# A selective-scan layer with a coupled feed-forward: gathers through DRAM, seven work slots, one gate per two phases, the norm's negated mean on ScalarE

## The chip, the cores and the metric

The kernel runs on one core of a Trainium2 chip. The metric is the device time of one execution in microseconds (us). Everything is float32. The engines are TensorE (PE), VectorE (DVE), ScalarE (ACT) and GpSimd (POOL); SyncE (SP) issues every DMA, in its own program order.

## The reference, cut to what matters

For each of 16 batch elements with 1024 time steps and 256 features: an input projection to 512 + 512 channels, a causal convolution of four taps, a selective scan with 16 states per channel, an output projection, a layer norm, three cycles of a small coupled network, and a second layer norm.

```
xi, res = split(x @ W_in.T + b_in);  xi = silu(conv4(xi) + b_conv)
proj  = xi @ W_x.T + b_x
delta = softplus(proj[:512]);  B, C = proj[512:528], proj[528:544]
h_t   = exp(-exp(A_log) * delta_t) * h_(t-1) + delta_t * B_t * xi_t     # 512 x 16 states, 1024 steps
y     = (sum_n h * C + xi * D) * silu(res)
x     = layernorm(x + y @ W_out.T + b_out)
out   = x;  3 times: out = out + coupling(out) * twist(out)
x     = layernorm(x + out)
```

## The kernel before, in words

**Tiling.** Channels lie on partitions. The 512 channels are DC = 4 blocks of 128, a block is QUAD = 4 groups of 32 channels. One *unit* handles 32 channels times 4 states, on 128 partitions (partition 32 n + i is state n of channel i), over all 1024 steps. Four units (j = 0 to 3, so 16 states) make a *phase*, four phases a block, and four blocks a *period* of 64 units, which is one batch element. There are 1024 units.

**A unit** runs through four engines. POOL makes `u_q * b_quad` into a slot of `work` (L944), ACT makes `da = exp(neg_a * delta_q)` (L721) into one of two PSUM buffers, DVE scans (L870), DVE or, for 24 units of a period, POOL two steps later multiplies by `c_quad` (L878, L951), and PE sums over the four states with the `fold` matrices into `y_sum` (L635). `work` has WORK = 5 slots, so POOL's unit t waits until PE has reduced unit t - 5. At the end of a phase DVE multiplies `y_sum` by silu(res) in `s_quad` (gate, L860); PE starts the next phase's sums (L626) only after that.

**Gathering.** The scan wants 32 channels repeated four times over the partitions. So for each phase SP copies 32 rows of `delta` and of `u = delta * xi` four times each, SBUF to SBUF (`copy_quads`, L338 and L344); three slots (COPIES) hold them. B and C go to DRAM once per period and are broadcast from there to b_quad and c_quad, 16 transfers each (L371), right at the change of period, into the buffers that the last phase still used. silu(res) comes from DRAM in four transfers per phase (L354), and the gated y goes in four transfers per phase to `yg` (L365), from where the output matmuls read.

**Around the units** run side tasks, at positions within the period written in tables: for the next batch element the projections x, r (L504, L519), the convolution v (L513), delta's projection d (L526), B and C (c); for the previous one the output matmuls o, transposes t, the network f and g, and the residual sum e. They share three PSUM banks, which a program assigns ahead (`assign_banks`); a task waits for the bank's former user. Every engine walks the same list t = FIRST ... END and does at each t its unit work and then its side tasks, strictly in order. ACT takes a task's result some positions later (X_TAKE, GELU1_AT and so on), and loads an activation table whenever the function changes (L657). `u` is made by POOL at DELTA_AT + U_LAG (L970). A norm is: DVE's bn_stats, bn_aggr and the negated mean (L846, L850, L853), then on ACT log, exp, shift and two applications (`normalise`, L665 to L676).

**SP** walks the list as well. At each t it may store y, load s_quad, copy the quads, store x1 (L420, at positions 9 and 12), reload x1 (L425), write out (L430), load x_res (L437), store res (L444), load x_feat, and the B and C loads. It waits for each one's data before it issues it, and nothing overtakes.

Of the kernel before, what the change touches and what calls it, by code (L numbers as in the profile page):

```python
# [30 lines left out]
WORK = 5  # L31
# [3 lines left out]
REDUCE_LAG = 1  # L35
# [32 lines left out]
F_AT = (0, 1, 1, 2, 3, 3, 5, 6, 7)  # L68
G_AT = (17, 19, 21)
E_AT = (59, 60, 61, 61)  # L70
# [60 lines left out]
def yg_position(g):  # L131

    return max(PHASE * (g + 1) + 1, PERIOD * (g // 16) + YG_AT)


def s_quad_position(g):

    return max(PHASE * (g - 2) + 1, yg_position(g - QUAD) if g >= QUAD else FIRST)
# [51 lines left out]
def build(nc, x, xT, weights, vectors, out):  # L190
    x1_dram = nc.dram_tensor("x1_scratch", [BATCH, SEQ, DM], F32, kind="Internal").ap()
    bc_dram = nc.dram_tensor("bc_scratch", [2 * NS, SEQ], F32, kind="Internal").ap()
    res_dram = nc.dram_tensor("res_scratch", [2, DC, P, SEQ], F32, kind="Internal").ap()

    with ExitStack() as ctx:
# [24 lines left out]
        yg = sb("yg", [P, DC, SEQ])  # L220
# [4 lines left out]
        neg_mean = sb("neg_mean", [P, 8, 2])  # L225
        log_var = sb("log_var", [P, 8, 2])
        r_std = sb("r_std", [P, 8, 2])
        shift = sb("shift", [P, 8, 2])
# [20 lines left out]
        def vs(name):  # L249
# [11 lines left out]
        bc_rows = soft[:, 0:QT]  # L261
# [18 lines left out]
        sq_in = [sem(f"s_quad_loaded{i}") for i in range(QUAD)]  # L280
        yg_in = [sem(f"yg_stored{i}") for i in range(QUAD)]
# [13 lines left out]
        o_ready, o_stat, o_mv, o_neg, o_log, o_rstd, o_shift, o_norm = (  # L295
            sem("o_" + n) for n in ("ready", "stat", "mv", "neg", "log", "rstd", "shift", "norm"))
        e_ready, e_stat, e_mv, e_neg, e_log, e_rstd, e_shift, e_norm = (
            sem("e_" + n) for n in ("ready", "stat", "mv", "neg", "log", "rstd", "shift", "norm"))
# [28 lines left out]
        def _(sp):  # L327
# [3 lines left out]
            def copy_quads(g):  # L331

                c, slot, m = g % QUAD, g % COPIES, g // QUAD
                sp.wait_ge(delta_ready, 2 * m + 2)
                if (before := g - COPIES) >= 0:
                    sp.wait_ge(da_ready, PHASE * before + PHASE)
                for n in range(QUAD):
                    sp.dma_start(delta_q[GROUP * n:GROUP * n + GROUP, slot, :],  # L338
                                 delta[GROUP * c:GROUP * c + GROUP, :]).then_inc(dq_in[slot], 16)
                sp.wait_ge(u_ready, m + 1)  # L340
                if before >= 0:
                    sp.wait_ge(dbx_ready, PHASE * before + PHASE)
                for n in range(QUAD):
                    sp.dma_start(u_q[GROUP * n:GROUP * n + GROUP, slot, :],  # L344
                                 u[GROUP * c:GROUP * c + GROUP, :]).then_inc(uq_in[slot], 16)

            def load_s_quad(g):

                b, m, c = g // 16, (g // QUAD) % DC, g % QUAD
                if g >= QUAD:  # L350
                    sp.wait_ge(yg_in[c], 64 * (g // QUAD))
                sp.wait_ge(res_stored, 16 * (DC * b + m + 1))
                for k in range(QUAD):
                    sp.dma_start(s_quad[GROUP * k:GROUP * k + GROUP, c, :],  # L354
                                 res_dram[b % 2, m, GROUP * c:GROUP * c + GROUP, QT * k:QT * k + QT]) \
                      .then_inc(sq_in[c], 16)

            def store_yg(g):

                b, m, c = g // 16, (g // QUAD) % DC, g % QUAD  # L360
                if m == 0 and c == 0 and b > 0:
                    sp.wait_ge(o_ready, 4 * b)
                sp.wait_ge(gated, g + 1)
                for k in range(QUAD):
                    sp.dma_start(yg[GROUP * c:GROUP * c + GROUP, m, QT * k:QT * k + QT],  # L365
                                 s_quad[GROUP * k:GROUP * k + GROUP, c, :]).then_inc(yg_in[c], 16)

            def load_rows(nb, j, tile, first, signal):

                for n in range(QUAD):  # L370
                    sp.dma_start(tile[GROUP * n:GROUP * n + GROUP, j, :],  # L371
                                 bc_dram[first + QUAD * j + n:first + QUAD * j + n + 1, :].partition_broadcast(GROUP)) \
                      .then_inc(signal[j], 16)

            def load_b(nb, j):
                sp.wait_ge(bc_stored, 64 * (nb + 1))
                if nb:
                    sp.wait_ge(dbx_ready, PERIOD * nb - PHASE + j + 1)
                load_rows(nb, j, b_quad, 0, b_in_)
# [17 lines left out]
            for t in range(FIRST, END):  # L397
                g, r, m = t // PHASE, t % PHASE, t // (4 * PHASE)
                if t % PERIOD == 0 and 0 <= t < UNITS:
                    load_c(t // PERIOD, 3)  # L400
# [623 lines left out]
```

## Time and profile before

| | us |
|---|---|
| median of 3 runs (4626.33 to 4634.05) | 4628.59 |
| the profiled execution | 4633.1 |
| its span, first to last instruction | 4631.3 |
| mean granted TensorE clock | 0.873 |
| busy: POOL, PE, DVE, ACT | 3648.9, 3639.7, 3565.9, 3059.8 |

The profile is of one execution. Its span is what the stages below add up to. A busy time is the time in which an engine had an instruction running. Where a row says "<-", it names what ended the idle time before the instruction.

### The profile page before, as it was taken

How to read it: one execution, taken by the hardware profiler on the slowest of the kernel's cores; microseconds unless marked ns; L12 is line 12 of the kernel's file. 1: busy time of each engine (PE TensorE's matmuls, PEld its weight loads, DVE VectorE, ACT ScalarE, POOL GpSimd, SP SyncE). 2: the span in 40 equal slices, each digit the busy share in tenths (PEclk: the TensorE clock that was granted, in tenths of full speed). 3: DMA queues.
4: the chain of work that ended last, by engine and by line, in shares of the span. 5: the costliest groups of instructions: out<-in, count | busy, mean ns of one | idle time of the engine just before them, and what ended most of it. 6: DMA issues, size and time to landing. Idle time of an engine off the chain costs nothing.

```text
span 4631.3 us, 53910 instructions
## 1 busy us (share of the span) xinstructions
PE 3639.7 (79%) x18112; PEld 1619.7 (35%) x18112; DVE 3565.9 (77%) x2784; ACT 3059.8 (66%) x3936; POOL 3648.9 (79%) x1602
## 2 busy tenths in 40 slices
PE   6668878788787877878688787887978788786765
PEld 2223343343333433343243433433333343433323
DVE  0887878888787887877788787887888788788871
ACT  2545857678585776858668485775858668585753
POOL 2987979889687887978879687887878879787871
PEclk8778988889898897988889898898988889898877
DMA  4454454634545444444634545445444634545430
GB/s 133 101 132 100 107 137 98 163 83 117 132 101 135 110 122 115 107 126 99 160 83 121 129 103 144 99 117 128 98 127 111 149 91 120 133 104 134 101 77 27
DMA packets 305603, 529.62 MB, mean 114 GB/s; under 512 B 77616, under 2 KB 210736, under 8 KB 305072
## 3 DMA queue, kind: packets, MB, share of 16 engines
q1 hardware_dynamic: 305328, 526.18, 46.4%
q8 instruction: 145, 2.38, 0.2%
q14 instruction: 130, 1.06, 0.1%
HBM read 154.67 MB, written 69.21 MB: 48 GB/s over the span
## 4 chain that ended last, share of the span: by engine, by line
ACT 26%; PE 25%; POOL 16%; SPq 11%; DVE 10%; issue 8%; DMA 3%; DVEq 0%; POOLq 0%; ACTq 0%
ACT L657 10%; POOL work L944 9%; ACT da L721 7%; PE banks L513 5%; DVE da L870 4%; POOL work L951 3%; PE banks L519 3%; SPq L371 3%; ACT big L692 3%; PE banks L504 3%; SPq L344 3%; DVE work L870 3%; SPq L338 3%; PE banks L593 3%; PE y_sum L635 3%
## 5 line engine op out<-in xcount | busy, mean ns | idle before, releaser
L944 POOL TENSOR_TENSOR work<-u_q,b_quad 128x1024 f32<-128x1024 f32 x1024 | 2394.6, 2359 | 424.6 <-DMA b_quad<-bc_scratch 194.8
L870 DVE TENSOR_TENSOR_SCAN da<-da,work 128x1024 f32<-128x1024 f32 x640 | 1465.4, 2290 | 355.8 <-ACT da L721 256.6
L721 ACT ACTIVATE da<-delta_q,neg_a 128x1024 f32<-128x1024 f32 x1024 | 1129.9, 1113 | 676.0 <-DVE work L878 572.5
L951 POOL TENSOR_TENSOR work<-work,c_quad 128x1024 f32<-128x1024 f32 x384 | 904.7, 2356 | 244.2 <-DVE work L870 242.3
L635 PE MATMUL y_sum<-work,v_all 128*32 128x256 f32 x8192 | 663.6, 430 | 417.2 <-DVE work L878 260.6
L878 DVE TENSOR_TENSOR work<-da,c_quad 128x1024 f32<-128x1024 f32 x640 | 782.4, 1223 | 211.7 <-DMA c_quad<-bc_scratch 191.0
L870 DVE TENSOR_TENSOR_SCAN work<-da,work 128x1024 f32<-128x1024 f32 x384 | 875.6, 2280 | 48.8 <-ACT da L721 48.3
L657 ACT ACT_TABLE_LOAD x575 | 737.7, 1283 | 35.9 <-DVE neg_mean L853 17.2
L635 PEld LDWEIGHTS y_sum<-work,v_all 128*32 128x32 f32 x8192 | 217.5, 116 | 894.3 <-DVE work L878 352.1
L526 PE MATMUL banks<-xi,w_all 128*128 128x512 f32 x1024 | 490.2, 629 | 15.7 <-ACT soft L816 12.7
L513 PE MATMUL banks<-xi,taps 128*128 128x512 f32 (+3 forms) x1024 | 458.1, 598 | 12.5 <-DVE big L895 11.7
L593 PE MATMUL banks<-oT,w_all 128*128 128x512 f32 x768 | 392.2, 647 | 39.0 <-ACT big L692 20.8
L504 PE MATMUL banks<-x_feat,w_all 128*128 128x512 f32 x512 | 311.0, 739 | 53.2 <-ACT xi L792 36.3
L665 ACT ACTIVATE log_var<-mean_var,eps_col 128x2 f32<-128x2 f32 x128 | 37.7, 295 | 422.7 <-DVE neg_mean L853 422.7
L526 PEld LDWEIGHTS banks<-xi,w_all 128*128 128x128 f32 x1024 | 197.0, 200 | 283.7 <-issue 254.1
L970 POOL TENSOR_TENSOR u<-delta,xi 128x1024 f32<-128x1024 f32 x64 | 151.0, 2360 | 160.8 <-DVE delta L907 160.8
L519 PE MATMUL banks<-x_feat,w_all 128*128 128x512 f32 x512 | 275.9, 672 | 1.1 <-DVE delta L907 1.1
L513 PEld LDWEIGHTS banks<-xi,taps 128*128 128x128 f32 x1024 | 189.0, 189 | 248.7 <-issue 228.7
L626 PE MATMUL y_sum<-xi,diag_d 128*32 128x256 f32 x2048 | 182.3, 431 | 116.4 <-DVE s_quad L860 116.4
L692 ACT ACTIVATE big<-banks,v_all 128x512 f32<-128x512 f32 x336 | 217.8, 684 | 58.7 <-PE banks L593 48.6
L548 PE MATMUL banks<-w_all,yg 128*128 128x256 f32 x1024 | 248.2, 386 | 5.3 <-DMA yg<-s_quad 5.3
L860 DVE TENSOR_TENSOR s_quad<-y_sum,s_quad 128x256 f32<-128x256 f32 x256 | 105.2, 411 | 161.0 <-PE y_sum L635 161.0
(71 smaller groups left out, 3542.3 us busy)
## 6 DMA issues: line engine op xcount, KB each, us to landing
delta_q<-delta SPq DMA_DIRECT2D x1024, 128.0 KB, 2.4
u_q<-u SPq DMA_DIRECT2D x1024, 128.0 KB, 2.5
res_scratch<-s_std SPq DMA_DIRECT2D x64, 512.0 KB, 3.3
s_quad<-res_scratch SPq DMA_DIRECT2D x1024, 32.0 KB, 1.9
b_quad<-bc_scratch SPq DMA_DIRECT2D x256, 128.0 KB, 3.0
c_quad<-bc_scratch SPq DMA_DIRECT2D x256, 128.0 KB, 3.9
yg<-s_quad SPq DMA_DIRECT2D x1024, 32.0 KB, 1.9
x_feat<-in_xT SPq DMA_DIRECT2D x16, 1024.0 KB, 5.5
```

The costliest lines, as they stand in the source:

```text
L504: mm = pe.matmul(banks[:, bank, :], w_in[:, k, m * P:m * P + P], x_feat[:, k, half * L:half * L + L], start=k == 0, stop=k == 1)
L513: mm = pe.matmul(banks[:, bank, to:], taps[:, m, k, :], xi[:, nb % 2, m, half * L + to - s:half * L + L - s], start=k == 3, stop=k == 0)
L519: mm = pe.matmul(banks[:, bank, :], w_in[:, k, DI + m * P:DI + m * P + P], x_feat[:, k, half * L:half * L + L], start=k == 0, stop=k == 1)
L526: mm = pe.matmul(banks[:, bank, :], w_x[:, k, m * P:m * P + P], xi[:, nb % 2, k, half * L:half * L + L], start=k == 0, stop=k == 3)
L593: mm = pe.matmul(shared, w1[:, k, m * P:m * P + P], oT[:, k, half * L:half * L + L], start=k == 0, stop=k == 1)
L635: mm = pe.matmul(y_sum[GROUP * i:GROUP * i + GROUP, 0:QT], fold, work[:, un % WORK, QT * i:QT * i + QT], start=False, stop=done)
L657: nc.scalar.preload_act_table_set(name)
L721: act.activation(da[:, t % 2, :], delta_q[:, slot, :], ACT.Exp, scale=neg_a[:, t % PERIOD:t % PERIOD + 1]).then_inc(da_ready, 1)
L870: dve.tensor_tensor_scan(dst, da[:, t % 2, :], work[:, slot, :], 0.0, ALU.mult, ALU.add) \
L878: dve.tensor_tensor(work[:, slot, :], da[:, t % 2, :], c_quad[:, j, :], ALU.mult).then_inc(prod_dve, 1)
L944: pool.tensor_tensor(work[:, slot, :], u_q[:, copied, :], b_quad[:, j, :], ALU.mult) \
L951: pool.tensor_tensor(work[:, un % WORK, :], work[:, un % WORK, :], c_quad[:, un % PHASE, :], ALU.mult) \
```

## The change

Delta and u are no longer copied within SBUF. Each is stored once per block to a DRAM scratch, and each phase loads its 32 rows four times over in one transfer; u shares its buffer with the softplus scratch `soft`. B, C, s_quad and y likewise take one transfer where they took four: B and C one per j, s_quad and y two per pair of phases. The gated y goes to DRAM, and `yg` is loaded from there, a quarter of the steps at a time, into two buffers. `work` has seven slots, PE takes POOL's products two units late, `y_sum` uses both halves of its bank and the gate runs once per two phases. The negated mean is made by ACT. SP's waits and all tables of positions are rewritten. Semaphore counts change from 64 to 16 where four transfers became one; such lines are left out here.

```diff
-WORK = 5
+WORK = 7
 COPIES = 3
 POOL_UNITS = ((1,), (0, 1))
 POOL_LAG = 2
-REDUCE_LAG = 1
+REDUCE_LAG = 2
...
-X_AT = (0, 2, 26, 27, 36, 38, 44, 49)
-V_AT = (4, 5, 28, 28, 40, 40, 53, 53)
-RES_AT = (2, 3, 27, 27, 38, 39, 47, 51)
-BC_AT = 55
-DELTA_AT = (7, 8, 2, 8)
-O_AT = (4, 9, 11, 11)
-T_AT = (13, 14, 15, 16)
+X_AT = (0, 0, 20, 25, 39, 39, 45, 49)
+V_AT = (2, 5, 28, 27, 42, 41, 51, 51)
+RES_AT = (0, 1, 26, 27, 39, 41, 47, 49)
+BC_AT = 54
+DELTA_AT = (8, 7, 3, 7)
+O_AT = (4, 7, 11, 12)
+T_AT = (15, 15, 16, 16)
 CYCLES = 3
 F_PER = 9
 CYCLE_AT = (16, 30, 44)
-F_AT = (0, 1, 1, 2, 3, 3, 5, 6, 7)
-G_AT = (17, 19, 21)
-E_AT = (59, 60, 61, 61)
+F_AT = (0, 1, 2, 2, 3, 4, 6, 7, 7)
+G_AT = (17, 18, 22)
+E_AT = (56, 58, 58, 61)
 
 X_TAKE = 3
 RES_TAKE = 3
-BC_TAKE = 3
+BC_TAKE = 2
 DELTA_TAKE, DELTA_MAX, U_LAG = 3, 3, 6
-O_STATS, O_NORM = 3, 4
-T_TAKE = 3
-GELU1_AT, GELU2_AT, GELU3_AT, GELU4_AT, TANH_AT = 3, 5, 6, 8, 9
+O_STATS, O_RS, O_NORM = 3, 4, 4
+T_TAKE = 2
+GELU1_AT, GELU2_AT, GELU3_AT, GELU4_AT, TANH_AT = 3, 5, 7, 9, 9
 MULT_AT, UPD_AT = 9, 11
-YG_AT = 14
-XRES_AT = 63
-SILU_AT = (10, 32, 46, 56)
+DST_AT, UST_AT = (11, 9, 13, 12), (11, 9, 5, 12)
+DLD_AT, ULD_AT = (13, 15, 16, 18), (13, 13, 18, 21)
+SLD, YST = -1, 2
+YGLD_AT = (3, 3, 7, 9)
+RESST_AT = (10, 31, 47, 54)
+X1ST_AT = (13, 13)
+RELOAD_AT, XRES_AT = 51, 64
+OUT_AT = (64, 72)
+XFEAT_AT = 55
+BCST_AT = 51
+LB_AT, LC_AT = (56, 57, 62, 62), (62, 62, 62, 64)
+SILU_AT = (9, 32, 45, 55)
...
+def batch_at(t, position):
+    f, rest = divmod(t - position, PERIOD)
+    return f if rest == 0 and 0 <= f < BATCH else None
+def block_at(t, table):
+    for ahead in range(3):
+        m = t // (4 * PHASE) + 1 - ahead
+        if 0 <= m < BATCH * DC and t == 4 * PHASE * (m - 1) + table[(m - 1) % DC]:
+            return m
+    return None
...
+    y_dram = nc.dram_tensor("y_scratch", [2, DC, P, SEQ], F32, kind="Internal").ap()
+    d_dram = nc.dram_tensor("delta_scratch", [2, P, SEQ], F32, kind="Internal").ap()
+    u_dram = nc.dram_tensor("u_scratch", [2, P, SEQ], F32, kind="Internal").ap()
...
-        s_quad = sb("s_quad", [P, QUAD, QT])
+        s_quad = sb("s_quad", [P, 2, 2, QT])
...
-        u = sb("u", [P, SEQ])
...
-        yg = sb("yg", [P, DC, SEQ])
+        yg = sb("yg", [P, 2, DC, QT])
...
-        bc_rows = soft[:, 0:QT]
+        u, bc_rows = soft, soft[:, 0:QT]
...
+            def store_delta(m):
+                sp.wait_ge(delta_ready, 2 * m + 2)
+                if m >= 2:
+                    for g in range(QUAD * (m - 2), QUAD * (m - 1)):
+                        sp.wait_ge(dq_in[g % COPIES], 16 * (g // COPIES + 1))
+                sp.dma_start(d_dram[m % 2], delta[:, :]).then_inc(d_stored, 16)
+            def store_u(m):
+                sp.wait_ge(u_ready, m + 1)
+                if m >= 2:
+                    for g in range(QUAD * (m - 2), QUAD * (m - 1)):
+                        sp.wait_ge(uq_in[g % COPIES], 16 * (g // COPIES + 1))
+                sp.dma_start(u_dram[m % 2], u[:, :]).then_inc(u_stored, 16)
+            def load_delta(g):
 
                 c, slot, m = g % QUAD, g % COPIES, g // QUAD
...
+                sp.wait_ge(d_stored, 16 * (m + 1))
+                if g >= COPIES:
+                    sp.wait_ge(da_ready, PHASE * (g - COPIES) + PHASE)
+                sp.dma_start(delta_q[:, slot, :], d_dram[m % 2, GROUP * c:GROUP * c + GROUP, :].unsqueeze(0)
+                             .broadcast_to([QUAD, GROUP, SEQ])).then_inc(dq_in[slot], 16)
+            def load_u(g):
+                c, slot, m = g % QUAD, g % COPIES, g // QUAD
+                sp.wait_ge(u_stored, 16 * (m + 1))
+                if g >= COPIES:
+                    sp.wait_ge(dbx_ready, PHASE * (g - COPIES) + PHASE)
+                sp.dma_start(u_q[:, slot, :], u_dram[m % 2, GROUP * c:GROUP * c + GROUP, :].unsqueeze(0)
+                             .broadcast_to([QUAD, GROUP, SEQ])).then_inc(uq_in[slot], 16)
+            def load_s_quad(pair):
+                b, m, c, slot = pair // 8, (pair // 2) % DC, 2 * (pair % 2), pair % 2
+                if pair >= 2:
+                    sp.wait_ge(y_stored[slot], 32 * (pair // 2))
                 sp.wait_ge(res_stored, 16 * (DC * b + m + 1))
...
+                for i in range(2):
+                    sp.dma_start(s_quad[:, slot, i, :],
+                                 res_dram[b % 2, m, GROUP * (c + i):GROUP * (c + i + 1), :]
+                                 .rearrange("p (k t) -> k p t", k=QUAD)).then_inc(sq_in[slot], 16)
+            def store_y(pair):
+                b, m, c, slot = pair // 8, (pair // 2) % DC, 2 * (pair % 2), pair % 2
+                sp.wait_ge(gated, pair + 1)
+                if b >= 2 and pair % 8 == 0:
+                    for i in range(2):
+                        sp.wait_ge(yg_in[i], 32 * (b - 1))
+                for i in range(2):
+                    sp.dma_start(y_dram[b % 2, m, GROUP * (c + i):GROUP * (c + i + 1), :]
+                                 .rearrange("p (k t) -> k p t", k=QUAD),
+                                 s_quad[:, slot, i, :]).then_inc(y_stored[slot], 16)
+            def load_yg(f, n):
+                i = 4 * f + n
+                for slot in range(2):
+                    sp.wait_ge(y_stored[slot], 32 * 4 * (f + 1))
+                if i >= 2:
+                    sp.wait_ge(o_ready, i - 1)
+                sp.dma_start(yg[:, n % 2, :, :],
+                             y_dram[f % 2, :, :, QT * n:QT * n + QT].rearrange("m p t -> p m t")).then_inc(yg_in[n % 2], 16)
+            def load_rows(j, tile, first, signal):
+                sp.dma_start(tile[:, j, :], bc_dram[first + QUAD * j:first + QUAD * j + QUAD, :].unsqueeze(1)
+                             .broadcast_to([QUAD, GROUP, SEQ])).then_inc(signal[j], 16)
 
             def load_b(nb, j):
...
+                sp.wait_ge(bc_stored, 16 * (nb + 1))
                 if nb:
                     sp.wait_ge(dbx_ready, PERIOD * nb - PHASE + j + 1)
...
+                load_rows(j, b_quad, 0, b_in_)
 
             def load_c(nb, j):
...
+                sp.wait_ge(bc_stored, 16 * (nb + 1))
                 if nb:
                     end = PERIOD * nb - PHASE + j
                     if by_pool(end):
                         sp.wait_ge(prod_pool, pool_products(end))
                     else:
                         sp.wait_ge(prod_dve, dve_products(end))
...
+                load_rows(j, c_quad, NS, c_in_)
...
+                ahead = t + PERIOD
+                if (t + SLD) % (2 * PHASE) == 0 and 0 <= (t + SLD) // (2 * PHASE) < 8 * BATCH:
+                    load_s_quad((t + SLD) // (2 * PHASE))
+                if (m := block_at(t, DST_AT)) is not None:
+                    store_delta(m)
+                if (m := block_at(t, UST_AT)) is not None:
+                    store_u(m)
+                for c in range(QUAD):
+                    if (m := block_at(t, (DLD_AT[c],) * DC)) is not None:
+                        load_delta(QUAD * m + c)
+                    if (m := block_at(t, (ULD_AT[c],) * DC)) is not None:
+                        load_u(QUAD * m + c)
+                if (t - YST) % (2 * PHASE) == 0 and 1 <= (t - YST) // (2 * PHASE) <= 8 * BATCH:
+                    store_y((t - YST) // (2 * PHASE) - 1)
+                for n in range(4):
+                    if (f := batch_at(t - PERIOD, YGLD_AT[n])) is not None:
+                        load_yg(f, n)
...
-                        if g:
-                            pe.wait_ge(gated, g)
+                        if g % 2 == 0 and g:
+                            pe.wait_ge(gated, g // 2)
...
-                act.activation(log_var[:, i, :], mean_var[:, i, :, 1], ACT.Ln, bias=eps_col[:, 0:1], scale=1.0) \
-                   .then_inc(log, 1)
+                act.activation(log_var[:, i, :], mean_var[:, i, :, 1], ACT.Ln, bias=eps_col[:, 0:1], scale=1.0)
+                act.activation(neg_mean[:, i, :], mean_var[:, i, :, 0], ACT.Identity, scale=-1.0).then_inc(log, 1)
...
-                dve.wait_ge(mv, n + 1)
-                dve.tensor_scalar(neg_mean[:, i, :], mean_var[:, i, :, 0], -1.0, 0.0, ALU.mult, ALU.add).then_inc(neg, 1)
...
+                slot = pair % 2
+                dve.wait_ge(reduced, phase_reduced(2 * pair + 1))
+                dve.wait_ge(sq_in[slot], 32 * (pair // 2 + 1))
+                dve.tensor_tensor(s_quad[:, slot, :, :], y_sum[:, :].rearrange("p (i t) -> p i t", i=2),
+                                  s_quad[:, slot, :, :], ALU.mult).then_inc(gated, 1)
...
+                    if m and half == 0:
+                        act.wait_ge(u_stored, 16 * m)
```

## Rows read from the trace of the kernel before

**Rows 1.** Page, part 1: busy us (share of the span) x instructions, per engine.

```profile
PE 3639.7 (79%) x18112; PEld 1619.7 (35%) x18112; DVE 3565.9 (77%) x2784; ACT 3059.8 (66%) x3936; POOL 3648.9 (79%) x1602
```

**Rows 2.** Page, part 4: the chain that ended last, by engine.

```profile
ACT 26%; PE 25%; POOL 16%; SPq 11%; DVE 10%; issue 8%; DMA 3%; DVEq 0%; POOLq 0%; ACTq 0%
```

**Rows 3.** Windows: length, busy (count) of PE, PEld, DVE, ACT, POOL; PEclk, DMA share, GB/s.

```profile
1723.50:1760.00 36.50, 18.65 (x84) 6.97 (x83) 19.38 (x22) 13.89 (x27) 18.83 (x9) 0.58 0.93 228
1760.00:2003.50 243.50, 207.92 (x1050) 93.75 (x1049) 202.12 (x152) 179.83 (x222) 208.73 (x90) 0.93 0.42 101
90.90:324.00 233.10, 154.16 (x832) 55.40 (x832) 197.26 (x125) 113.50 (x123) 210.15 (x91) 0.77 0.51 119
4244.00:4485.00 241.00, 160.09 (x873) 68.17 (x873) 206.11 (x151) 154.60 (x191) 215.45 (x94) 0.75 0.43 103
```

**Rows 4.** Timelines of POOL and DVE at a period's start: waits in brackets.

```profile
1726.49 2.36 POOL L944 TENSOR_TENSOR work<-u_q,b_quad 128x1024 f32<-128x1024 f32 x1 [5.20 <-DMA b_quad<-bc_scratch]
1735.13 2.34 POOL L944 TENSOR_TENSOR work<-u_q,b_quad 128x1024 f32<-128x1024 f32 x1 [6.28 <-DMA b_quad<-bc_scratch]
1740.93 2.34 POOL L944 TENSOR_TENSOR work<-u_q,b_quad 128x1024 f32<-128x1024 f32 x1 [3.46 <-DMA b_quad<-bc_scratch]
...
1732.80 1.22 DVE L878 TENSOR_TENSOR work<-da,c_quad 128x1024 f32<-128x1024 f32 x1 [5.06 <-DMA c_quad<-bc_scratch]
1750.32 1.23 DVE L878 TENSOR_TENSOR work<-da,c_quad 128x1024 f32<-128x1024 f32 x1 [7.35 <-DMA c_quad<-bc_scratch]
```

**Rows 5.** Waits from 1760 to 2003.5: us in total, times, longest.

```profile
DVE da L870 <- ACT da L721: 16.3, 12, 3.8
DVE s_quad L860 <- PE y_sum L635: 8.1, 5, 3.5
...
POOL work L944 <- PE y_sum L635: 8.6, 4, 4.5
POOL work L944 <- DMA u_q<-u: 5.1, 1, 5.1
...
ACT soft L829 <- DMA bc_scratch<-soft: 4.6, 1, 4.6
```

**Rows 6.** Page: DMA packets; issues, with us to landing.

```profile
DMA packets 305603, 529.62 MB, mean 114 GB/s; under 512 B 77616, under 2 KB 210736, under 8 KB 305072
...
res_scratch<-s_std SPq DMA_DIRECT2D x64, 512.0 KB, 3.3
s_quad<-res_scratch SPq DMA_DIRECT2D x1024, 32.0 KB, 1.9
```

**Rows 7.** SP's timeline: four issues.

```profile
1583.37 2.42 SPq L338 DMA_DIRECT2D delta_q<-delta  x4
```

**Rows 8.** SP's waits in one period, longest first.

```profile
SPq L420 <- ACT big L676: 37.4, 1, 37.4
```

**Rows 9.** Windows (columns as in rows 3): copies alone, then DRAM transfers alone.

```profile
1642.00:1644.00 2.00, 2.00 (x6) 0.95 (x5) 2.00 (x2) 0.96 (x1) 2.00 (x2) 1.00 0.93 207
1694.00:1696.00 2.00, 1.28 (x24) 0.35 (x16) 2.00 (x3) 1.99 (x2) 2.00 (x2) 1.00 1.08 406
```

**Rows 10.** POOL's timeline at a change of block: u, then units.

```profile
1712.03 2.35 POOL L970 TENSOR_TENSOR u<-delta,xi 128x1024 f32<-128x1024 f32 x1
1718.95 2.34 POOL L944 TENSOR_TENSOR work<-u_q,b_quad 128x1024 f32<-128x1024 f32 x1
```

**Rows 11.** Groups by line: busy us, mean ns, then idle before.

```profile
L657 ACT ACT_TABLE_LOAD x575 | 737.7, 1283 | 35.9 <-DVE neg_mean L853 17.2 <-DMA bc_scratch<-soft 4.0 <-DMA v_all<-in_vectors 3.6
L860 DVE TENSOR_TENSOR s_quad<-y_sum,s_quad 128x256 f32<-128x256 f32 x256 | 105.2, 411 | 161.0 <-PE y_sum L635 161.0
L853 DVE TENSOR_SCALAR neg_mean<-mean_var 128x2 f32<-128x2 f32 x128 | 102.7, 803 | 4.4
L907 DVE SCALAR_TENSOR_TENSOR delta<-banks,v_all,soft 128x512 f32<-128x512 f32 x128 | 95.0, 742 | 149.3 <-ACT soft L835 149.3
L671 ACT ACTIVATE shift<-neg_mean,r_std 128x1 f32<-128x1 f32 x256 | 61.4, 287 | 4.2
```

More of the change, by code:

```diff
@@ L279, in build @@
         res_stored = sem("res_stored")
-        sq_in = [sem(f"s_quad_loaded{i}") for i in range(QUAD)]
-        yg_in = [sem(f"yg_stored{i}") for i in range(QUAD)]
+        d_stored, u_stored = sem("delta_stored"), sem("u_stored")
+        sq_in = [sem(f"s_quad_loaded{i}") for i in range(2)]
+        y_stored = [sem(f"y_stored{i}") for i in range(2)]
+        yg_in = [sem(f"yg_loaded{i}") for i in range(2)]
         x1_stored = [sem(f"x1_stored{i}") for i in range(2)]
@@ L347, in load_s_quad @@
[L347 to L351, printed above, removed]
-                sp.wait_ge(res_stored, 16 * (DC * b + m + 1))
[L353 to L356, printed above, removed]
@@ L435, in _ @@
+                for h in range(2):
+                    if (f := batch_at(t - PERIOD, OUT_AT[h])) is not None:
+                        sp.wait_ge(e_norm, 4 * f + 2 * h + 2)
+                        sp.dma_start(out[f, h * L:(h + 1) * L, :].rearrange("(k p) c -> p k c", p=P),
+                                     x1[:, 4 * h:4 * h + 4, :]).then_inc(out_done[h], 16)
+                if (f := batch_at(t, XRES_AT)) is not None:
                     if f:
@@ new lines, in _ @@
+                for n in range(DC):
+                    if (nb := batch_at(ahead, RESST_AT[n])) is not None:
+                        sp.wait_ge(res_ready, DC * nb + n + 1)
+                        sp.dma_start(res_dram[nb % 2, n], s_std[:, :]).then_inc(res_stored, 16)
+                if (nb := batch_at(ahead, XFEAT_AT)) is not None and nb + 1 < BATCH:
+                    sp.wait_ge(r_ready, 8 * nb + 8)
+                    load_x_feat(nb + 1)
+                if (nb := batch_at(ahead, BCST_AT)) is not None:
+                    for j in range(PHASE):
+                        if nb:
+                            sp.wait_ge(c_in_[j], 16 * nb)
+                            sp.wait_ge(b_in_[j], 16 * nb)
+                    sp.wait_ge(c_taken, nb + 1)
+                    sp.dma_start(bc_dram.rearrange("r (k t) -> k r t", k=QUAD), bc_rows).then_inc(bc_stored, 16)
@@ L463, in _ @@
+                for j in range(PHASE):
+                    if (nb := batch_at(ahead, LB_AT[j])) is not None:
+                        load_b(nb, j)
+                    if (nb := batch_at(ahead, LC_AT[j])) is not None:
+                        load_c(nb, j)
             for h in range(2):
@@ L539, in couple @@
                 if kind == "o":
+                    pe.wait_ge(yg_in[n % 2], 16 * (2 * f + n // 2 + 1))
                     if n == 0:
-                        for c in range(QUAD):
-                            pe.wait_ge(yg_in[c], 64 * DC * (f + 1))
                         pe.wait_ge(xr_in, 16 * (f + 1))
@@ L547, in couple @@
                         for k in range(4):
-                            pe.matmul(half, yg[:, k, tb * P:tb * P + P], w_out[:, k, :], start=k == 0, stop=False)
+                            pe.matmul(half, yg[:, n % 2, k, r * P:r * P + P], w_out[:, k, :], start=k == 0, stop=False)
                         pe.matmul(half, eye, b_out, start=False, stop=False)
@@ L903, in _ @@
                     if m and half == 0:
-                        for i in range(COPIES):
-                            last = QUAD * m - COPIES + i
-                            dve.wait_ge(dq_in[last % COPIES], 64 * (last // COPIES + 1))
+                        dve.wait_ge(d_stored, 16 * m)
                     dve.scalar_tensor_tensor(out=delta[:, cols],
@@ L965, in _ @@
                     pool.wait_ge(xi_ready, 8 * (m // DC) + 2 * (m % DC) + 2)
-                    if m:
-                        for i in range(COPIES):
-                            last = QUAD * m - COPIES + i
-                            pool.wait_ge(uq_in[last % COPIES], 64 * (last // COPIES + 1))
                     pool.tensor_tensor(u[:, :], delta[:, :], xi[:, (m // DC) % 2, m % DC, :], ALU.mult).then_inc(u_ready, 1)
```

164 lines of the change are left out of this document (39 added, 125 removed).

## The prediction

> **What bounds the kernel now.** I read the busy shares first. They name no single engine: POOL 79%, PE 79%, DVE 77%, ACT 66% [rows 1], and the chain of waits is spread over all of them with 11% on SP's queue [rows 2]. So I went to the stages. One period (64 units, one batch element) lasts 280.0 us; in it POOL is busy 227.6, PE 226.6, DVE 221.5 and ACT 193.7 us (each the sum of the first two rows of [rows 3]). From 324 to 4244 us there are 3920/280 = 14 such periods; before them lie a start of 90.9 and a first period of 233.1 us, after them a last period of 241.0 us [rows 3] and, up to the span's end at 4631.3, a tail of 146.3.
>
> Within a period two stretches differ. The first phase (units 0 to 3) takes 36.5 us, the other fifteen 243.5, that is 16.2 each [rows 3]. In the first phase POOL waits 5.20, 6.28 and 3.46 us for b_quad, DVE 5.06 and 7.35 us for c_quad [rows 4]. In the others DVE waits 16.3 us for ACT's da and 8.1 for PE's sums before the gate; POOL waits 8.6 us for a work slot that PE has not reduced and 5.1 for u_q [rows 5].
>
> Behind the DMA waits stands SP's queue. 4851 transfers (303 a period) go out on it [rows 6], four for each gather at about 0.6 us a piece: 2.42 us for one delta_q [rows 7], so roughly 180 us of a period. It also works in order: for 37.4 us it stands before the x1 store (L420) until ACT's norm is done [rows 8], everything behind it late. The gathers themselves are slow too: SBUF to SBUF they move 207 GB/s at a DMA share of 0.93, DRAM transfers (reload, then a res store) 406 GB/s at 1.08 [rows 9].
>
> **Part 1, fewer issues.** After, a period issues 16 + 4 delta, 16 + 4 u, 16 s_quad, 16 y, 4 yg, 4 b, 4 c, 1 bc and 11 others = 96 instead of 303. SP falls to some 50 us, and the x1 stores stand behind the loads of the next block. This alone would remove the first phase's excess (36.5 − 16.2 = 20 us) and the 5.1 us for u_q.
>
> **Part 2, how wide a gather runs.** This decides the case. In the old form the leading dimension of every transfer is 32 or 128 rows. The page counts 77616 packets under 512 B [rows 6], and 77616/4851 = 16 exactly: each transfer closes with sixteen small packets, one per DMA engine, so each was split over all sixteen. The new gathers of delta, u, b and c have on the DRAM side a leading dimension of QUAD = 4 (unsqueeze(0).broadcast_to([4, 32, 1024]), or four rows each broadcast), and s_quad and y have "k p t" with k = 4. No row of before has a leading dimension under 16, so the trace bounds the price only from both sides. At 16 engines 0.524 MB take 0.524/406 = 1.3 us [rows 9]; at four, 406/4 = 101.5 GB/s, 5.2 us. I take four: sixteen equal shares along the leading dimension is what every observed transfer got, and a dimension of four can't be cut so. Both ends stay for the range.
>
> The Trainium skill, "DMA: Bandwidth & Descriptors", section "Rules for kernel authors", says the same and against this change: an outermost dimension below 16, its example being a leading zero-stride broadcast, confines the whole transfer to that many engines; its section on why a semaphore goes up by 16 adds that on SP's queue these are the lowest-numbered ones. No transfer here shows that; by it the sum is the one below, without it the first rival.
>
> Load on those four engines per period, if they are the same four: 40 gathers of 0.524 MB and 32 of 0.131 MB = 25.2 MB at 101.5 GB/s = 248 us. The 16-wide ones (12 stores of delta, u and res, 4 yg, and 5.2 MB of x_feat, x_res, reload, x1 and out: 13.6 MB) at 406 GB/s add 34. Together 282 us: the four engines alone need as much as a period lasts today.
>
> **Part 3, the new hand-off.** delta and u go out to DRAM and come back, and the load waits for the store's semaphore. A 512 KB store lands in 3.3 us [rows 6]. From the end of u: issue 0.4, store landed 3.7; meanwhile the delta gather, next in SP's order, holds the four engines until 1.3 + 5.2 = 6.5; then the u gather until 11.7, receipt about 2 (the landing of a small transfer, 1.9 [rows 6]): 13.6 us. POOL needs it two steps later. Today u ends at 1714.38 and the first unit of the next block starts at 1718.95 [rows 10]: 4.6 us of cover where u is made at offset 14, about twice that at offset 13. The new DELTA_AT (8, 7, 3, 7) puts u at offsets 14, 13, 9, 13: stalls of about 9, 4 and 0 us for three blocks, and with the gather queue behind them (delta, u, u, then delta, delta) I take 10, 6 and 0.
>
> The fourth block ends the period, and there b and c come on top. When POOL has finished unit 61, the queue before c of j = 3 holds b1, the delta and u stores, delta 0, u0, u1, b2, b3, c0, c1, c2, delta 1, c3: eleven gathers × 5.2 + 2.6 = 60 us. DVE needs c3 for unit 67, some 8.5 units or 32 us later: a stall of about 30, for which I put 32. At sixteen engines the same queue takes 17 us and nobody waits.
>
> **Part 4, the pace between the stalls.** WORK 7 ends POOL's 8.6 us wait for reduced slots. The gate falls from 16 × 0.411 us [rows 11] to 8 × about 0.74 (the nearest row, a 128x512 PSUM read, L907 [rows 11]), and PE stands before it half as often: about 4 of 8.1 us. The negated mean leaves DVE, 102.7/16 = 6.4 us a period, and costs ACT 8 × 0.29 = 2.3 [rows 11], where ACT has been waiting for that very result. GELU4 and tanh now share a position: five table switches and returns per cycle become four, 6 × 1.28 = 7.7 us of ACT [rows 11], less up to 1.2 us three times for the matmul between them; of DVE's 16.3 us behind ACT I take 4. c is taken two positions earlier, which covers ACT's 4.6 us wait for the bc store [rows 5]. REDUCE_LAG 2 lets PE ask for POOL's products a unit later; bounds 0 to 3 us, I take 3. The new positions of E spread the four tasks, so that the fourth no longer asks for the bank of the first before ACT has emptied it; I count nothing for that, since PE's lateness there is covered by the first phase's other waits. In sum 4 + 6.4 + 4 + 3 = 17.4 us: (243.5 − 17.4)/15 = 15.1 us a phase. Below 227.6/16 = 14.2 it can't go, since POOL is busy that long. The shared soft/u buffer adds a wait of ACT for the u store, made some ten units earlier: nothing, unless the store queues behind gathers. Loading yg from DRAM adds one landing before the output matmuls, covered by four units.
>
> **The sum.** 16 × 15.1 = 241 us of pace, plus 10 + 6 + 0 + 32 = 289. The four DMA engines need 282 and idle in the part of a block where no slot is free, so the two limits don't overlap wholly: I take 295. Start 91 + 20 (eleven gathers of the first block, 57 us, partly behind preparation) = 111; first period 233 − 10 + 24 = 247; 14 × 295 = 4130; last 241 − 8 + 34 = 267; tail 150. Together 4905. The profiled execution took 4633.1 us for its span of 4631.3; the median shown is 4628.6, 4.5 lower. That gives 4900. Own range: pace at POOL's floor with the DMA limit, 285 a period, 4760, less 5% for packets faster than the one row I price them by, 4550; pace as today, 16.2, and full stalls, 307 a period, 5070, and some more for SP held at issue by full queues, 5300.
>
> **Rivals.** (1) The gathers run on all sixteen engines, and the gain comes through: the place is SP's queue at the period's end, the price 20 us there, 5.1 for u_q and 17.4 of pace, less about 3 for the hand-off at offset 14 (0.4 + 3.3 + 0.4 + 3.5 − 4.6). A period of 280 − 20 − 5 − 17 + 3 + some 6 that other waits take back = 247; 14 × 247 + 92 + 225 + 222 + 143 = 4140 to 4190, taken as 4180. It decides from the width on: it needs at least about eight engines, since then the four-wide 248 us fall to 124. For it: the 406 GB/s and SP's 180 us; against it: the leading dimension. Chance 0.12. (2) Sixteen engines, but only the boundary and u_q are gained, the pace stays with PE, DVE and POOL as tightly coupled as now: 4631 − 16 × 20 + 16 × 2 = 4345. Chance 0.05. (3) Four engines, but the gained pace pays for the stalls: 227 + 48 = 275 to 280 a period, 4630. It needs POOL without any other wait and the DMA limit 2% below my 282. Chance 0.03. The forecast has 0.80.
>
> Changes within 0.2% (9 us) can't be told from none here. Faster: rivals 1 and 2 less a little, 0.15; same 0.02; slower 0.83. The range 4550 to 5300 holds most of the forecast's 0.80 and rival 3.
>
> **What would show it.** Packets under 512 B: 1168 narrow and 371 wide transfers make 4 × 1168 + 16 × 371 = 10608 if four, 24624 if sixteen. The mean DMA share sits near 0.25 to 0.35 with seldom a full slice, though the engines in use are full; a 512 KB gather lands in 7 us or more instead of 3 to 4. POOL's largest wait is DMA u_q, DVE's DMA c_quad, together above 40 us a period; POOL's wait for PE y_sum nearly vanishes, L853 is gone, table loads fall by about 90. Granted clock falls with PE's idle time. If u_q and c_quad waits are small, part 2 is wrong and rival 1 holds; if gathers are slow but the period is near 280, the hand-off arithmetic of part 3 is.

## The result and the profile after

The changed kernel takes 5830.42 us (median of 4 runs, 5828.52 to 5835.52) against 4627.65: 1.2597 times as long, 95% interval 1.2576 to 1.2619. The direction was as forecast; 5830 lies outside the range of 4550 to 5300.

The page after, its busy shares, the chain by engine, and the packets:

```profile
PE 3696.3 (63%) x18112; PEld 1680.4 (29%) x18112; DVE 3464.7 (59%) x2528; ACT 2952.5 (51%) x3974; POOL 3644.7 (62%) x1602
DMA 25%; POOL 24%; SPq 17%; issue 14%; PE 9%; DVE 5%; ACT 5%; POOLq 0%; DVEq 0%; ACTq 0%
DMA packets 287719, 629.79 MB, mean 108 GB/s; under 512 B 10608, under 2 KB 176496, under 8 KB 287216
```

Every engine does what it did [rows 1] and waits more; the chain has moved to DMA and SP [rows 2]. 10608 packets under 512 B are what the forecast gave for four engines per gather; sixteen would give 24624.

Windows (columns as in [rows 3]): one period, and ten microseconds inside it.

```profile
1825.00:2180.00 355.00, 229.23 (x1132) 104.77 (x1132) 216.54 (x159) 186.75 (x250) 227.29 (x99) 0.81 0.32 110
...
2180.00:2190.00 10.00, 2.67 (x17) 0.90 (x18) 5.23 (x8) 0.59 (x3) 1.72 (x1) 0.50 0.26 105
```

A period went from 280 to 355 us with POOL busy 227.3. In the second row the DMA share is 0.26 of sixteen engines, that is four full ones, and they move 105 GB/s (I had 101.5), while ACT and POOL nearly stand still. Such a share looks like idle DMA, but the four that are in use are full. Counted from the packets in the trace, over ten periods from 1000 us on, at least four packets are in flight for 298 of a period's 355 us and none for 44.

Waits of the whole span (us in total, times, longest):

```profile
POOL work L981 <- DMA u_q<-u_scratch: 872.3, 97, 23.4
ACT da L762 <- DMA delta_q<-delta_scratch: 812.1, 80, 22.9
POOL work L988 <- DVE work L909: 447.6, 101, 14.1
POOL work L981 <- DMA b_quad<-bc_scratch: 375.9, 32, 16.4
DVE work L917 <- DMA c_quad<-bc_scratch: 340.1, 48, 17.1
ACT log_var L706 <- DMA out<-big: 324.6, 15, 22.7
POOL work L981 <- PE y_sum L676: 196.9, 15, 14.2
```

POOL idles 355 − 227 = 128 us a period. By the sums above, divided by the 16 periods, it waits 54.5 us for u_q, 23.5 for b_quad, 28.0 for DVE's scan and 12.3 for PE; some 10 are left for the rest. Before it idled 52 us.

POOL's timeline from the third block of a period, over the change of period, to the first change of block after it:

```profile
2018.59 9.26 POOL L981 TENSOR_TENSOR work<-u_q,b_quad 128x1024 f32<-128x1024 f32 x4 [9.75 <-DMA u_q<-u_scratch]
...
2067.85 6.98 POOL L981 TENSOR_TENSOR work<-u_q,b_quad 128x1024 f32<-128x1024 f32 x3 [2.94 <-DMA u_q<-u_scratch]
...
2088.85 9.27 POOL L981 TENSOR_TENSOR work<-u_q,b_quad 128x1024 f32<-128x1024 f32 x4 [7.10 <-DMA u_q<-u_scratch]
...
2140.64 4.66 POOL L981 TENSOR_TENSOR work<-u_q,b_quad 128x1024 f32<-128x1024 f32 x2 [4.53 <-DMA u_q<-u_scratch]
2145.24 2.36 POOL L1003 TENSOR_TENSOR soft<-delta,xi 128x1024 f32<-128x1024 f32 x1
...
2177.09 4.63 POOL L981 TENSOR_TENSOR work<-u_q,b_quad 128x1024 f32<-128x1024 f32 x2 [20.24 <-DMA u_q<-u_scratch]
2197.28 2.34 POOL L981 TENSOR_TENSOR work<-u_q,b_quad 128x1024 f32<-128x1024 f32 x1 [15.56 <-DMA b_quad<-bc_scratch]
2207.38 2.34 POOL L981 TENSOR_TENSOR work<-u_q,b_quad 128x1024 f32<-128x1024 f32 x1 [7.76 <-DMA b_quad<-bc_scratch]
...
2232.08 2.34 POOL L988 TENSOR_TENSOR work<-work,c_quad 128x1024 f32<-128x1024 f32 x1 [13.16 <-DVE work L909]
...
2259.75 2.36 POOL L981 TENSOR_TENSOR work<-u_q,b_quad 128x1024 f32<-128x1024 f32 x1 [13.83 <-PE y_sum L676]
...
2286.05 2.36 POOL L1003 TENSOR_TENSOR soft<-delta,xi 128x1024 f32<-128x1024 f32 x1
...
2303.47 9.26 POOL L981 TENSOR_TENSOR work<-u_q,b_quad 128x1024 f32<-128x1024 f32 x4 [10.44 <-DMA u_q<-u_scratch]
```

L1003 makes u. At the change of block it ends at 2286.05 + 2.36 = 2288.41, and the first unit of the next block starts 15.1 us later, when its u has landed (landing forecast after 13.6; before, the unit started after 4.6 [rows 10]). At the change of period this takes 29.5 us.

SP's timeline at the change of period (start, length of the issue, what, count), and two rows of the page's issues with their size and median time to landing:

```profile
2164.02 1.14 SPq L382 DMA_DIRECT2D u_q<-u_scratch  x2
2165.25 8.22 SPq L420 DMA_DIRECT2D c_quad<-bc_scratch  x2
2173.56 4.80 SPq L420 DMA_DIRECT2D b_quad<-bc_scratch  x1
2178.46 4.80 SPq L420 DMA_DIRECT2D c_quad<-bc_scratch  x1
2183.35 4.80 SPq L420 DMA_DIRECT2D b_quad<-bc_scratch  x1
2188.24 10.79 SPq L373 DMA_DIRECT2D delta_q<-delta_scratch  x2
2199.08 4.96 SPq L477 DMA_DIRECT2D out<-big  x1
...
res_scratch<-s_std SPq DMA_DIRECT2D x64, 512.0 KB, 11.7
oT<-in_x SPq DMA_DIRECT2D x16, 1024.0 KB, 19.7
```

Two gathers go out in 1.14 us. Then each issue takes 4.1 to 5.4 us, about the time of one gather on four engines (0.524 MB at 105 GB/s is 5.0), and the sixteen-wide out store at the end takes as long: SP stands inside the issue. Over the period from 1825 to 2180 the issues of 96 transfers take SP 203 us in its timeline; before, some 180 us went to 303 transfers. What runs on sixteen engines can wait for the busy four as well: a res store lands in 11.7 us instead of 3.3 [rows 6], but a u store in 2.9.

### The profile page after: what moved, and what is told of

Read it like the earlier page. It is cut to its first block, busy times and chain, and to the rows that moved or that the text cites. A ratio compares the mean times of both kernels' runs of the same rounds, so it can differ in the third digit from the quotient of the medians.

```text
span 5833.7 us, 50294 instructions
## 1 busy us (share of the span) xinstructions
PE 3696.3 (63%) x18112; PEld 1680.4 (29%) x18112; DVE 3464.7 (59%) x2528; ACT 2952.5 (51%) x3974; POOL 3644.7 (62%) x1602
## 2 busy tenths in 40 slices
DMA packets 287719, 629.79 MB, mean 108 GB/s; under 512 B 10608, under 2 KB 176496, under 8 KB 287216
## 4 chain that ended last, share of the span: by engine, by line
DMA 25%; POOL 24%; SPq 17%; issue 14%; PE 9%; DVE 5%; ACT 5%; POOLq 0%; DVEq 0%; ACTq 0%
POOL work L981 14%; DMA u_q<-u_scratch 8%; SPq L420 7%; DMA c_quad<-bc_scratch 6%; POOL work L988 5%; DMA res_scratch<-s_std 5%; DMA u_scratch<-soft 4%; SPq L373 4%; DMA delta_scratch<-delta 2%; SPq L404 2%; DVE da L909 2%; POOL soft L1003 2%; POOL oT L997 2%; ACT L698 2%; PE banks L633 2%
## 5 line engine op out<-in xcount | busy, mean ns | idle before, releaser
L698 ACT ACT_TABLE_LOAD x485 | 622.3, 1283 | 33.3 <-DVE mean_var L890 16.9
L667 PE MATMUL y_sum<-xi,diag_d 128*32 128x256 f32 x2048 | 198.7, 467 | 677.0 <-DVE s_quad L898 677.0
L588 PE MATMUL banks<-w_all,yg 128*128 128x256 f32 x1024 | 300.2, 445 | 321.6 <-issue 239.8
L554 PE MATMUL banks<-xi,taps 128*128 128x512 f32 (+3 forms) x1024 | 494.0, 630 | 0.1
L633 PE MATMUL banks<-oT,w_all 128*128 128x512 f32 x768 | 417.8, 690 | 85.0 <-ACT xi L848 66.9
L588 PEld LDWEIGHTS banks<-w_all,yg 128*128 128x128 f32 x1024 | 223.9, 225 | 391.1 <-issue 275.4
L667 PEld LDWEIGHTS y_sum<-xi,diag_d 128*32 128x32 f32 x2048 | 51.9, 123 | 843.3 <-DVE s_quad L898 733.4
## 6 DMA issues: line engine op xcount, KB each, us to landing
res_scratch<-s_std SPq DMA_DIRECT2D x64, 512.0 KB, 11.7
```

The source lines that it names most:

```text
L554: mm = pe.matmul(banks[:, bank, to:], taps[:, m, k, :], xi[:, nb % 2, m, half * L + to - s:half * L + L - s], start=k == 3, stop=k == 0)
L588: pe.matmul(half, yg[:, n % 2, k, r * P:r * P + P], w_out[:, k, :], start=k == 0, stop=False)
L633: mm = pe.matmul(shared, w1[:, k, m * P:m * P + P], oT[:, k, half * L:half * L + L], start=k == 0, stop=k == 1)
L698: nc.scalar.preload_act_table_set(name)
```

## The experiments

**Width or path.** The rival to the width was that the way through DRAM, or SP's order, costs the time. First the partition order of the scan is changed so that the same single transfers lead with 32 (edit shortened).

```
-  d_dram[...32 rows].unsqueeze(0).broadcast_to([QUAD, GROUP, SEQ])       # u the same
+  d_dram[...32 rows].unsqueeze(1).broadcast_to([GROUP, QUAD, SEQ])
-  bc_dram[...4 rows].unsqueeze(1).broadcast_to([QUAD, GROUP, SEQ])
+  bc_dram[...4 rows].unsqueeze(0).broadcast_to([GROUP, QUAD, SEQ])
   # fold and the order of A_log rearranged to partition = 4 * channel + state
```

> The changed kernel with one thing different: the scan's partition order is 4 * channel + state instead of 32 * state + channel. Each gather of delta, u, b and c is still one transfer, but its DRAM side now leads with 32 instead of 4. Theory (width): a transfer runs on only as many DMA engines as its leading dimension allows, always the same first ones; here delta, u, b and c run on sixteen, s_quad and y stay on four. The small packets count 16 x 755 + 4 x 784 = about 13 to 16 thousand, a gather lands in 3 to 5 us, a period takes 245 to 270 instead of 355 us: 4150 to 4450 us, faster than before. Rival (path): the round trip through DRAM and SP's strict order cost the time, whatever the width: the time stays at 5600 to 5900 us.

Measured: 4435.13 us, ratio 0.9578 (0.9562 to 0.9594), faster than before. Small packets 18288 = 16 × 1011 + 4 × 528 (my count in the expectation was too low). One permutation of partitions is worth 1395 us, with the same path and the same number of issues; the path is not the cause.

**More issues, same width.** Four transfers of 32 rows for each gather:

> The changed kernel with each gather of delta, u, b and c issued as four transfers of 32 rows from DRAM (leading dimension 32), the partition order unchanged. Theory (width): as wide as the one with the other partition order, but with 120 more issues a period on SP (about 60 us of its time): 4200 to 4550 us. Rival (issues): if it is the number of issues that counts and not the width, this is no better than the changed kernel's 5830 us, since it takes issues back that the change removed.

Measured: 4667.96 us (one run), 118 above the range of my theory and far below the rival's 5830. Width recovers most of it here too. Against the single wide transfers it costs 233 us more, 14.6 a period. That is not the price of 120 more issues alone, since a transfer of 32 rows is slower as well. Here are two microseconds at the change of period with the engines full, mostly of gathers, in this run and then in the run with single wide transfers:

```profile
1733.00:1735.00 2.00, 0.00 (x0) 0.00 (x0) 2.00 (x2) 0.00 (x0) 1.42 (x1) 0.50 1.02 225
...
1644.00:1646.00 2.00, 0.00 (x0) 0.00 (x0) 0.97 (x1) 0.00 (x0) 2.00 (x2) 0.50 1.02 406
```

At the same DMA share the four-part gathers move 225 GB/s, the single ones 406. No run separates this from the issues, so what fewer issues are worth by themselves stays open.

**The narrow loads alone, in the kernel before** (edit shortened):

```
-  for n in range(QUAD): sp.dma_start(tile[32n:32n+32, j, :], bc_dram[row n].partition_broadcast(GROUP))
+  sp.dma_start(tile[:, j, :], bc_dram[4 rows].unsqueeze(1).broadcast_to([QUAD, GROUP, SEQ]))
```

> The kernel before with its b_quad and c_quad loads alone turned into one transfer each with a leading dimension of four (128 of them instead of 512), nothing else. Theory (width): eight transfers of 5.2 us on four engines fall into the first phase of each period, where the DMA queue was already full: 10 to 25 us more a period, 4780 to 5030 us; 69936 small packets. Rival (issues): SP has 24 fewer issues a period just where it is late, so the first phase gets shorter: 4500 to 4600 us.

Measured: 4926.74 us (one run) against 4628.37, and exactly 69936 small packets: 18.6 us a period for eight narrow loads, although 24 issues a period are saved. POOL's wait for b_quad goes from 194.8 to 489.3 us, DVE's for c_quad from 191.0 to 501.8.

**Narrower still, and on which engines.** Each delta and u gather as two transfers that lead with 2:

> The changed kernel with each delta and u gather as two transfers of 64 partitions whose DRAM side leads with 2. Theory (width, and always the same first engines): these run on engines 0 and 1 alone, which then have 32 x 0.524 MB at 51 GB/s = 331 us a period, plus 82 for b, c, s_quad and y and 34 for the wide ones, about 450; at the same utilisation as the changed kernel's (0.88) 510 us a period, 8000 to 8900 us. Rival (narrow transfers are spread over the sixteen engines in turn, only the landing is late): load stays balanced, 5900 to 6500 us. Rival (path): 5700 to 6000 us.

Measured: 8048.06 us (one run), as the width with fixed engines says. A window of that run, in which SP issues gathers of this form:

```profile
3000.00:3010.00 10.00, 0.00 (x0) 0.00 (x0) 0.00 (x0) 2.15 (x2) 0.00 (x0) 0.50 0.13 52
```

DMA share 0.13 is two full engines, and they move 52 GB/s. Several transfers in flight don't spread over more engines, so they use the same two.

**Total load or hand-off.** By 105 GB/s I estimate the four engines' load at 25.2/0.105 = 240, plus 34 for the wide transfers, 274 of 355 us; the packets give 298. Is it the amount that bounds? s_quad and y are made wide by another DRAM layout, everything else as changed (edit shortened):

```
-  res_dram, y_dram: [2, DC, P, SEQ], s_quad and y in two transfers "p (k t) -> k p t"
+  res_dram, y_dram: [2, DC, QUAD, QUAD, GROUP, QT], one transfer "i k p t -> (k p) i t", res and yg in four of 32 rows
```

> The changed kernel (delta, u, b and c still four wide) with s_quad and y alone made sixteen wide by the same layout. It takes 32 of 306 us a period of load off the four engines' queues net of nothing on the hand-off itself. Theory (load: the four engines bound the kernel, 306 of 355 us busy): the period falls by 30 to 45 us, 5100 to 5400 us. Rival (hand-off: the stalls come from the latency of the delta and u gathers after each block and of b and c, not from the total): 0 to 10 us a period, 5670 to 5830 us. 18800 small packets.

Measured: 5654.34 us (one run), 11 a period less, 18800 small packets. That lies between the two, nearer to the hand-off. (The 306 there was my estimate from packet durations.) By the packets, at least four are now in flight for 271 of 344 us. So 27 us of load went and 11 came back: the amount counts for a part, the order of the hand-offs for more.

**Which gathers.** Each pair of gathers is made wide by itself:

> The changed kernel with the delta and u gathers in four transfers of 32 rows each (sixteen wide), b and c still four wide, s_quad and y too. Against the run with all of them split (4668 us). Theory (b and c narrow cost at the change of period what they cost in the kernel before, 18.6 us a period): 4930 to 5000 us, so delta and u are worth 830 to 900 of the changed kernel's excess. Rival (the change of period carries most of the missing time): over 5300 us.

> The changed kernel with b and c in four transfers each (sixteen wide), delta, u, s_quad and y still four wide. Theory (delta and u are the larger part): 5400 to 5650 us, 12 to 27 us a period below the changed kernel. Rival (the change of period carries most of it, 49 us a period measured from u's end to unit 68 beyond the pace): below 5200 us.

Measured: 5102.59 us with delta and u wide, 5526.86 with b and c wide (one run each). With 5830 (none wide) and 4668 (both wide) this is a square. Narrow delta and u cost 859 us when b and c are wide and 727 when they are narrow (54 and 45 a period); narrow b and c cost 435 and 303 (27 and 19). Each costs more alone than on top of the other, so they share stalls. All four numbers are net of the slower transfers of 32 rows and the added issues, so the width itself is worth more. The second expectation came in. In the first run both missed: b and c cost more here than in the kernel before (18.6), but far from most.

**A store behind a load.** OUT_AT (64, 72) made (64, 66), first in the kernel with wide gathers, then in the changed one:

> The kernel with the channel-major partition order (all gathers of delta, u, b and c sixteen wide) and one position changed: the second half of the output is stored at 66 instead of 72, ahead of the third yg load, so that ACT's first norm of the next batch element no longer waits for it (14 us a period in the run before this). Theory (that wait is on the path): 10 to 14 us a period come off, 4435 falls to 4210 to 4290 us. Rival (another wait takes its place, since PE's output matmuls and POOL are late at the same spot): 4380 to 4440 us.

Measured: 4351.33 us (one run), outside both ranges: 5 of the 14 us a period come off, and another wait takes the rest.

> The changed kernel (gathers four wide) with the second output store at 66 instead of 72. Theory (of its 355 us a period some 20 are ACT waiting before the first norm for that store, held behind the third yg load): 12 to 20 us a period off, 5510 to 5640 us. Rival (SP stands anyway while the four engines' queues are full, and the store moved ahead holds yg and s_quad instead): 5750 to 5850 us.

Measured: 5750.33 us (one run), also 5 a period, of 20. ACT's 324.6 us wait for the output store was mostly a place where time showed, not where it was lost.

**All wide.** The early store and the wide s_quad and y together:

> As the kernel with the earlier output store, and the small transfers made sixteen wide too: res and y lie in DRAM as [group, time quarter, channel, time], so s_quad and y take one transfer with leading dimension 128 per pair of phases, res stores and yg loads four of 32 rows. Packets under 512 B: sixteen per transfer. Theory (the four engines are now a third loaded and only delay what queues behind them): 1 to 3% below the kernel without it, 4130 to 4260 us. Rival (nothing waits for the small ones): the same within 0.5%.

Measured: 4225.52 us, ratio 0.9127 (0.9111 to 0.9142); 126 us (2.9%) below the run with the early store alone. Its page, one period, and two of its waits:

```profile
PE 3496.8 (83%) x18112; PEld 1614.3 (38%) x18112; DVE 3449.5 (82%) x2528; ACT 2945.6 (70%) x3974; POOL 3647.2 (86%) x1602
...
1579.50:1832.20 252.70, 215.43 (x1140) 99.49 (x1132) 215.56 (x159) 186.10 (x250) 226.76 (x98) 0.93 0.47 155
...
POOL work L981 <- DMA u_q<-u_scratch: 49.5, 21, 8.1
POOL work L981 <- DMA b_quad<-bc_scratch: 40.3, 32, 3.2
```

A period takes 252.7 us with POOL busy 226.8, and the granted clock is 0.93 instead of the 0.88 before [rows 3]. SP's issues take some 66 us of it, for 105 transfers.

**The other parts, undone one at a time.** Seven slots to five (in the first wide kernel), and in the all-wide one the mean back on DVE, REDUCE_LAG back to 1, and the network's positions of before:

> The channel-major kernel with five work slots instead of seven. Theory (the longer ring lets PE lag behind and is worth the wait of POOL for reduced slots, 8.6 us a period in the kernel before): 2 to 5% slower, 4520 to 4660 us. Rival (POOL is held within two units of DVE by its own product anyway, so the slots beyond five are hardly used): within 1% of 4435 us.

Measured: 4515.53 us (one run) against 4435.13, 1.8% slower, just under my range: 5 us a period for two slots.

> The all-wide kernel with the negated mean back on DVE. Theory (the norm's move is worth DVE's 0.17 to 4.4 us per instruction, 6.4 us a period, and part of it is on the path): 3 to 7 us a period more, 4270 to 4340 us. Rival (DVE has slack beside ACT's da there, and ACT is spared 2.3 us a period): 4210 to 4245 us, no difference from 4225.

Measured: 4273.99 (two runs, 4273.53 and 4274.45): the norm's move is worth 48 us, 3 a period.

> The all-wide kernel with REDUCE_LAG back at 1: PE asks for each POOL product one unit earlier and stands before it with all its side tasks. Theory (that wait holds PE's side tasks and with them ACT): 2 to 6 us a period, 4255 to 4320 us. Rival (with seven slots PE's place does not matter): 4210 to 4245 us.

Measured: two runs, 4230.03 and 4237.98, overlap with 4217 to 4233: no difference shown, as the rival said.

> The all-wide kernel with the network's positions of before: GELU3 at 6, GELU4 at 8, tanh at 9, and F_AT as before, so five table switches per cycle instead of four (about 90 table loads more, 575 in all, 119 us of ACT). Theory (ACT bounds these stretches: DVE's largest wait is ACT's da): 3 to 7 us a period, 4270 to 4340 us. Rival (ACT's extra loads fall into its idle time): within 0.5% of 4225 us.

Measured: 4389.09 (4387.10 and 4391.09), 164 us or 10 a period, more than I expected. There are 575 table loads of 1283 ns against 485: 115 us, so more is lost than ACT's own time, by the positions or by what waits for ACT; DVE's wait for ACT's da rises from 197.8 to 252.6 us and POOL's for DVE's scan from 153.6 to 310.2.

**The third block's delta, stored early:**

> The all-wide kernel with the third block's delta stored at offset 4 of its block instead of 13, ahead of the u store. Theory (its gather waited for that store, 123 us of SP's waiting in all, and the u gather behind it): 1 to 3 us a period, 4175 to 4215 us. Rival (the waits there are hidden behind the pace): 4215 to 4235 us, no difference.

Measured: 4217.23 us (4216.48 to 4220.62), ratio 0.9111 (0.9096 to 0.9127). It is 8 us or 0.2% below, within the other's spread: no difference shown.

## Why the prediction was wrong, step by step

- **Bound before, and the gain on offer:** right in kind. The first rival was priced at 4140 to 4190. The all-wide kernel, which also has the earlier output store, takes 4217 to 4225, some 30 us above that. With the output store where the change has it and s_quad and y narrow, the wide gathers give 4435.
- **Part 2, width four on fixed engines:** right, by the packet count, by 0.26 at 105 GB/s, and by the permutation that removes it. By that rule of the Trainium skill ("DMA: Bandwidth & Descriptors", "Rules for kernel authors"), the runs agree: leading dimensions of 32, 4 and 2 gave sixteen, four and two engines.
- **Part 1, "SP falls to some 50 us":** wrong. The issues take 203 us. I priced an issue at its time in a queue with room. Behind full engines one takes 4.1 to 5.4 us, and SP holds everything behind it.
- **Part 3 is the step that failed, by its size.** The mechanism was right, late gathers after each block and at the change of period. The stalls were too small: 10 + 6 + 0 us for delta and u after three blocks, and 32 at the change of period, 48 in all. In the timeline of POOL it waits for u_q 10.4, 9.8 and 7.1 us at the three changes of block and 2.9 and 4.5 us inside blocks, 35 against 16. At the change of period it waits 20.2 us for u_q, 15.6 and 7.8 for b_quad and 13.2 for DVE, which waited for c_quad: 57 against 32. The single hand-off was nearly right (15.1 against 13.6). Missing was that the gathers inside a block are late too, since SP issues them late, that the third block waits as well, and that the wide transfers, which I gave landing times from an empty queue, stand behind the narrow ones.
- **"Covered by four units"** for the yg load: wrong. SP issues it only when the y store before it, itself four wide, has landed, and PE's output matmuls wait 15.9 us, POOL behind them 13.8. ACT's norm waits for the output store, which stands behind the third yg load; with that store moved ahead 5 us a period come back. The rows are SP's waits before the yg load in total, the two issues, and PE's wait.

```profile
SPq L414 <- DMA y_scratch<-s_quad: 155.4, 15, 11.5
...
2225.17 8.04 SPq L404 DMA_DIRECT2D y_scratch<-s_quad  x2
2244.03 0.91 SPq L415 DMA_DIRECT2D yg<-y_scratch  x2
...
2247.59 3.75 PE L588 MATMUL banks<-w_all,yg 128*128 128x256 f32 x8 [15.86 <-issue]
```

- **The sum of these:** 19 us at and inside the blocks, 25 at the change of period and 14 behind yg make 58 of the 66 us by which a period of 355 exceeds the 289 of pace and stalls in my sum (295 with the two limits). The other 8 are in smaller waits.
- **Part 4, the pace:** about right. 252.7/16 = 15.8 us a phase in the all-wide kernel with its remaining waits, against 15.1. Its pieces: the slots are worth 5 us (I named 8.6 of POOL's wait and put none of it into the sum), the norm 3 (6.4 for DVE), the network's positions 10 (4), REDUCE_LAG 0 (3). The gate once per two phases (4) was not undone by itself.
- **The two limits:** I took 295 as little above the engines' 282. By the packets the engines were in use for 298 of 355 us, a little more than my 282. But they were not the whole bound: of 27 us of load taken off, only 11 came back.
- **A reading of [rows 9]:** I put the 207 GB/s of the old copies down to their path from SBUF to SBUF. Gathers of 32 rows from DRAM move 225 GB/s at a share of 1.02, the same per busy engine. So the path is not what made the old copies slow; 32 rows a transfer is what both have in common.

Not settled: how the 355 us divide between SP standing at issue and the gathers' own landing. Both come from the same full queues, and no run separates them.

## What to carry to other kernels

Before merging DMAs, look at the leading dimension of both sides: here a merge that turned 32 into 4 left four engines of sixteen, 105 GB/s instead of 406. Afterwards, count the packets under 512 B per issue: 16, 4 or 2 tell the width. A different partition order can keep the merge and the width. A low mean DMA share with a constant level (0.26, 0.13) is a few full engines, not room.

## What the runs showed of the hardware

- SP's issue of a DMA is short only at first: 0.57 us each for two gathers, then 4.1 to 5.4 us each while the engines work off what was issued. It also happens sixteen wide, in the burst at the change of period of the all-wide kernel: 5.15 us for two c_quad issues. How much may be in flight before it starts was not measured.
- Transfers of 32 rows moved 225 GB/s with all engines busy, transfers of 128 rows 406, both from DRAM.
- The negated mean of 128x2 elements took DVE 0.17 to 4.36 us. In the kernel before, 45 of the 128 took over 0.3 us, and every one of them ended within 0.05 us of the end of a POOL instruction; none of the other 83 lies inside one. One of the 45 (1717.23 + 1.78 and 1716.65 + 2.34, both 1719.0):

```profile
1717.23 1.78 DVE L853 TENSOR_SCALAR neg_mean<-mean_var 128x2 f32<-128x2 f32 x1
1716.65 2.34 POOL L951 TENSOR_TENSOR work<-work,c_quad 128x1024 f32<-128x1024 f32 x1
```

The Trainium skill, "SBUF — State Buffer", section "SBUF: two separate sides", says that a DVE operation in one of its two-port modes and a GpSimd operation take turns on a shared pair of ports, each for its whole instruction; this trace agrees, in that the short operation ends only with POOL's. It would explain why so small an operation was worth moving, 48 us here.
